# Values of all tokens projected token-major in the first stage, four groups at a time, by way of a scratch in memory; both ends of the last stage reordered

## The reference, cut to what matters

```python
q = (x @ Wq.T).reshape(B, L, H, D)             # x is the normalised input, H = 32, D = 128
k = (x @ Wk.T).reshape(B, L, KVH, D)           # KVH = 8
v = (x @ Wv.T).reshape(B, L, KVH, D)
q, k = _apply_rope(q, cos, sin), _apply_rope(k, cos, sin)
dt = softplus(x @ Win.T + dt_bias); g = dt * -exp(A_log_bias)
G = cumsum(g over a chunk)
scores = q_i . k_j                              # within a chunk of 128 tokens
y_intra = (scores * causal exp(G_i - G_j)) @ (v * dt)
y_inter = (q * exp(G)) @ state before the chunk
state = state * exp(G_last) + (k * exp(G_last - G)).T @ (v * dt)
y = rms_norm(y_intra + y_inter) * gnorm_w * silu(x @ Wg.T)
x1 = x + y @ Wo.T
out = x1 + dense(layer_norm(x1)) + experts(layer_norm(x1))
```

## Time and profile before

| | us |
|---|---|
| median of 3 runs (lowest, highest) | 1906.51 (1904.37, 1909.8) |
| the profiled execution, device time | 1906.53 |
| its span | 1904.7 |
| PE busy | 1824.3 (96%) |
| DVE busy | 1272.7 (67%) |
| ACT busy | 692.1 (36%) |
| POOL busy | 645.5 (34%) |
| mean granted TensorE clock | 0.984 |

### The profile page before, as it was taken

How to read it: one execution, slowest core, us unless ns; L and a number is a source line. 1 busy time by engine, 2 the same in 40 slices (tenths; PEclk the granted TensorE clock), 3 DMA queues, 4 the chain that set the end, 5 groups by cost and what they waited for, 6 DMA issues and landing times. The chain is left out here.

```text
span 1904.7 us, 27787 instructions
## 1 busy us (share of the span) xinstructions
PE 1824.3 (96%) x8856; PEld 1481.1 (78%) x8856; DVE 1272.7 (67%) x2340; ACT 692.1 (36%) x2186; POOL 645.5 (34%) x741
## 2 busy tenths in 40 slices
PE   6799999999999999999999999999887999999997
PEld 4578878877877888787788878888676888888885
DVE  7777877787787778787777868888764333333332
ACT  4534444443344344344444433443442211111111
POOL 3444444444444444444444444444301011010110
PEclk9899999999999999999999999999998999999998
DMA  4132332233233223332322333322364232322321
GB/s 156 46 104 78 99 95 68 71 101 93 82 93 95 70 69 104 96 86 84 95 74 65 106 91 83 87 68 72 129 214 134 82 100 79 98 83 82 100 79 32
DMA packets 111073, 173.54 MB, mean 91 GB/s; under 512 B 8016, under 2 KB 45904, under 8 KB 110928
## 3 DMA queue, kind: packets, MB, share of 16 engines
q1 hardware_dynamic: 110928, 171.80, 30.7%
HBM read 133.50 MB, written 38.27 MB: 90 GB/s over the span
## 5 line engine op out<-in xcount | busy, mean ns | idle before, releaser
L84 PE MATMUL p_proj<-wg_hi,shared 128*128 128x512 f32 x1024 | 360.8, 433 | 0.0
L84 PE MATMUL p_proj<-shared,wq_hi 128*128 128x512 f32 x992 | 335.3, 399 | 0.0
L113 POOL TENSOR_TENSOR q<-rope_a,rope_b 128x512 f32<-128x512 f32 x128 | 166.7, 1302 | 339.7 <-DVE rope_b L105 209.4
L84 PEld LDWEIGHTS p_proj<-wg_hi,shared 128*128 128x128 f32 x1024 | 193.7, 189 | 85.0 <-issue 40.2
L917 ACT ACTIVATE tanh<-p_proj 128x512 f32<-128x512 f32 x128 | 76.5, 598 | 444.8 <-PE p_proj L84 444.8
L84 PEld LDWEIGHTS p_proj<-shared,wq_hi 128*128 128x128 f32 x992 | 186.4, 188 | 44.7 <-issue 1.6
L84 PE MATMUL p_proj<-wg_lo,shared 128*128 128x512 f32 x512 | 203.2, 397 | 0.0
L84 PE MATMUL p_proj<-shared,wq_lo 128*128 128x512 f32 x496 | 196.1, 395 | 0.0
L910 ACT ACTIVATE probs<-g_row,stab 128x128 f32<-128x128 f32 x512 | 164.0, 402 | 54.9 <-POOL g_row L1024 54.8
L694 PE MATMUL p_y<-v_tok,probs 128*128 128x128 f32 x1024 | 182.1, 275 | 0.0
L84 PE MATMUL p_proj<-shared,wkv_hi 128*128 128x512 f32 x496 | 171.4, 407 | 0.0
(11 more groups left out here) (181 smaller groups left out, 3755.5 us busy)
## 6 DMA issues: line engine op xcount, KB each, us to landing
g_row<-g_scratch SPq DMA_DIRECT2D x128, 256.0 KB, 6.0
z_scratch<-z_st SPq DMA_DIRECT2D x256, 128.0 KB
w_raw<-z_scratch SPq DMA_DIRECT2D x63, 512.0 KB, 6.5
e_row<-e_scratch SPq DMA_DIRECT2D x96, 256.0 KB, 4.1
w_raw<-in_wq_t SPq DMA_DIRECT2D x16, 512.0 KB, 8.0
w_raw<-in_wg_t SPq DMA_DIRECT2D x16, 512.0 KB, 5.6
w_raw<-in_wo_t SPq DMA_DIRECT2D x11, 512.0 KB, 5.8
w_raw<-in_wkv_t SPq DMA_DIRECT2D x8, 512.0 KB, 5.1
```

The costliest lines, as they stand in the source:

```text
L84: mm = pe.matmul(out, lhs[a], rhs[e], start=(i == 0 and j == 0), stop=(i == len(pairs) - 1 and j == 2))
L113: pool.tensor_tensor(out, keep["rope_a"][:, s, :], keep["rope_b"][:, s, :], ALU.add).then_inc(keep["roped"], 1)
```

## The change

V is no longer a unit of every attention step. The first stage multiplies each token tile by the V weights of four groups (512 columns) and then by those of the other four, 32 units of 12 matmuls with the tokens on the output's partitions (`values`), saved by ACT (`save_v`) and stored to a scratch in memory (`v_dram`) by SP. The attention stage loads V of a batch and group (256 KB) into one of two buffers, a step ahead (`load_v`); the V unit, `v_turn`, `save_v_rows` and `save_v` of each step are gone. K's weights are loaded and split alone. The first stage's order of loads, splits, table chain and projections is new on all engines, and both tables share one PSUM bank. In the last stage x of tile 0 is loaded first, the last two heads of tile 1 come behind the transposes of tile 0, the splits of W come behind the normalising of tile 0, and `dense` comes behind `turn_hw` and the next tile's heads.

```diff
+        TABLES = 4
+
+        V_LAG, TABLES_AT = 3, 9
+
+        def v_place(v):
+            if v >= 2 * NT - 2:
+                return (keep["k"][:, 1, :], v_tok[:, 1, :, :].rearrange("p c d -> p (c d)"))[v - (2 * NT - 2)]
+            return xin[:, v, :] if v < NT - 2 else v_rows[v % 4]
+
+
+        early_out, place_out = sem("n_early_out"), [sem(f"n_place_out{i}") for i in range(4)]
+
+        def v_count(v):
+            return early_out if v < NT - 2 else place_out[v % 4] if v < 2 * NT - 2 else v_out
...
+            def store_v(v):
+                half, i = v // NT, v % NT
+                sp.wait_ge(v_set, v + 1)
+                sp.dma_start(v_dram[half * HG:(half + 1) * HG, i].rearrange("g s d -> s g d"),
+                             v_place(v).rearrange("p (g d) -> p g d", g=HG)).then_inc(v_count(v), 16)
...
+            for i in (1, 2):
+                sp.dma_start(part(w_raw, i), half_piece(io["wv_t"], 0, i)).then_inc(wv_in[0], 16)
...
             load_x(1)
+            load_x(2)
+            load_x(3)
...
+            sp.dma_start(part(w_raw, 0), k_piece(io, 0)).then_inc(k_in, 16)
+            sp.dma_start(keep["cos"][:, :], io["cos_t"]).then_inc(trig_in, 16)
+            sp.dma_start(keep["sin"][:, :], io["sin_t"]).then_inc(trig_in, 16)
+            sp.wait_ge(wv_lo, 2)
+            for i in (1, 2):
+                sp.dma_start(part(w_raw, i), half_piece(io["wv_t"], 1, i)).then_inc(wv_in[1], 16)
+            for v in range(8):
+                store_v(v)
+            sp.wait_ge(w_lo, 2)
             for i in (1, 2):
                 sp.dma_start(part(w_raw, i), half_piece(io["wq_t"], 0, i)).then_inc(q_in, 16)
-            sp.dma_start(keep["cos"][:, :], io["cos_t"]).then_inc(trig_in, 16)
-            sp.dma_start(keep["sin"][:, :], io["sin_t"]).then_inc(trig_in, 16)
-            sp.wait_ge(w_lo, 3)
+            for v in range(8, NT):
+                store_v(v)
+            sp.wait_ge(w_lo, 5)
             for i in (1, 2):
                 sp.dma_start(part(w_raw, i), half_piece(io["wg_t"], 0, i)).then_inc(g_in, 16)
+            for v in range(NT, NT + TABLES):
+                store_v(v)
             sp.wait_ge(G_set, 1)
             sp.dma_start(g_dram.rearrange("c b g h t -> (b g h) c t"), G[:, :].rearrange("h (c t) -> h c t", t=C)).then_inc(g_out, 16)
             sp.wait_ge(eg_set, 1)
             sp.dma_start(e_dram.rearrange("c b g h t -> (b g h) c t"), eg[:, :].rearrange("h (c t) -> h c t", t=C)).then_inc(g_out, 16)
+            for v in range(NT + TABLES, 2 * NT):
+                store_v(v)
             sp.wait_ge(g_out, 32)
+
+            for i in range(4):
+                sp.wait_ge(place_out[i], 16 * NT // 4)
...
+            w_low(2, wv[1], 1)
+            w_low(3, wv[1], 2)
+            w_low(4, wk, 0)
+            w_low(5, wq, 1)
+            w_low(6, wq, 2)
             add_rope(pool, keep, 0, 0, 0)
-            add_rope(pool, keep, 0, 0, 1)
-            w_low(3, wg, 1)
-            add_rope(pool, keep, 0, 0, 2)
-            w_low(4, wg, 2)
...
                         low_part(i - 2)
-                    if i == 11:
-                        dve.wait_ge(trig_in, 32)
-                        rotate_tile(0)
+                    if i == V_LAG:
+                        for h in (1, 2):
+                            dve.wait_ge(w_hi, h)
+                            dve.tensor_tensor(dst(wv[0][1], h), part(w_raw, h), dst(wv[0][0], h).bitcast(F32),
+                                              ALU.subtract).then_inc(wv_lo, 1)
...
+            def save_v(v):
+                act.wait_ge(v_done, v + 1)
+                if NT + 2 <= v < 2 * NT - 2:
+                    act.wait_ge(place_out[v % 4], 16 * ((v - (NT - 2)) // 4))
+                if v in (NT - 2, NT - 1, NT, NT + 1):
+                    act.wait_ge(xt_done, NT)
+                act.activation(v_place(v), pv[v % 2][:, :], ACT.Copy).then_inc(v_set, 1)
+
             for i in range(NT):
                 halves(i)
-
...
+                if i == 0:
+                    w_high(wv[0], 1, wv_in[0], 32)
+                    w_high(wv[0], 2, wv_in[0], 32)
                 if i == 9:
-                    w_high(wq, 2, q_in, 32)
-                if i == 13:
-                    act.wait_ge(unit_done, 2)
-                    act.activation(keep["v_t"][:, :], p_proj[1][:, :, :].rearrange("p h t -> p (h t)"), ACT.Copy).then_inc(v_set, 1)
+                    w_high(wv[1], 1, wv_in[1], 32)
+                    w_high(wv[1], 2, wv_in[1], 32)
+                if i == 11:
+                    w_high(wk, 0, k_in, 16)
+                    act.wait_ge(small_in, 16 * 2 * B)
+                    act.activation(hcol[:, 2:3], hcol[:, 1:2], ACT.Exp).then_inc(acol_set, 1)
+                if i >= V_LAG:
+                    save_v(i - V_LAG)
+            for v in range(NT - V_LAG, NT):
+                save_v(v)
             act.wait_ge(dt_done, NT)
+            act.wait_ge(early_out, 16 * (NT - 2))
...
-            w_high(wg, 1, g_in, 32)
+            save_v(NT)
             act.wait_ge(u1_set, 1)
...
-            w_high(wg, 2, g_in, 32)
+            save_v(NT + 1)
             act.wait_ge(dt_up_set, 1)
             act.activation(ln_dt[:, :], dt_up[:, :], ACT.Ln).then_inc(ln_dt_set, 1)
+            save_v(NT + 2)
+            w_high(wq, 1, q_in, 32)
+            w_high(wq, 2, q_in, 32)
+            save_v(NT + 3)
             act.wait_ge(G_set, 1)
...
+            for v in range(NT + 4, NT + TABLES_AT):
+                save_v(v)
+            w_high(wg, 1, g_in, 32)
+            w_high(wg, 2, g_in, 32)
             for j, k in enumerate((T_BIAS, T_W)):
                 act.wait_ge(tabs_done, j + 1)
-                act.activation(tab[:, :, k, :], ptab[k][:, :, :], ACT.Copy).then_inc(tabs_saved, 1)
+                act.activation(tab[:, :, k, :], ptab[:, :, :], ACT.Copy).then_inc(tabs_saved, 1)
+            for v in range(NT + TABLES_AT, 2 * NT):
+                save_v(v)
...
+            def values(v):
+                half, i = v // NT, v % NT
+                if i == 0:
+                    if half:
+                        pe.wait_ge(w_lo, 2)
+                    else:
+                        pe.wait_ge(wv_lo, 2)
+                pe.wait_ge(lo_set, i + 1)
+                if v >= 2:
+                    pe.wait_ge(v_set, v - 1)
+                wide(pe, pv[v % 2][:, :], [(x_parts(keep, i // NC, kt, slice(i % NC * P, (i % NC + 1) * P)),
+                                            (wv[half][0][:, kt, :], wv[half][1][:, kt, :])) for kt in range(KT)]).then_inc(v_done, 1)
+
+            def project_tile(r):
+                if r == 0:
+                    pe.wait_ge(w_lo, 3)
+                    pe.wait_ge(lo_set, NC)
+                if r == 1:
+                    pe.wait_ge(w_lo, 5)
+                if r >= 2:
+                    pe.wait_ge(rope_terms, r - 1)
+                project(pe, keep, *((wq, (r - 1) * D) if r else (wk, 0)), 0, p_proj[r % 2]).then_inc(unit_done, 1)
 
             for i in range(NT):
                 turn(i)
                 if i:
                     dt_rows(i - 1)
-                if i == 9:
-                    pe.wait_ge(w_lo, 1)
-                    pe.wait_ge(lo_set, NC)
-                    project(pe, keep, wkv, 0, 0, p_proj[0]).then_inc(unit_done, 1)
-                if i == 12:
-                    project(pe, keep, wkv, D, 0, p_proj[1]).then_inc(unit_done, 1)
+                if i >= V_LAG:
+                    values(i - V_LAG)
             dt_rows(NT - 1)
-            pe.wait_ge(w_lo, 3)
-            for h in range(HG):
-                project_q(h)
+            for v in range(NT - V_LAG, NT + TABLES_AT):
+                values(v)
             for k in (T_BIAS, T_W):
                 turn_table(k)
+            for r in range(ROPED):
+                project_tile(r)
+                values(NT + TABLES_AT + r)
+            for v in range(NT + TABLES_AT + ROPED, 2 * NT):
+                values(v)
...
-        BANKS = (0, 1, 2, 1, 0, 2, 1, 0, 2, 1)
+        BANKS = (0, 1, 2, 0, 1, 2, 0, 1, 2)
...
+            def load_v(g, b):
+                sp.dma_start(v_tok[:, b % 2], v_dram[bass.ds(g, 1), b * NC:(b + 1) * NC].rearrange(
+                    "a c s d -> s (a c) d")).then_inc(v_in[b % 2], 16)
...
+                if ahead(n):
+                    if has_last(n):
+                        sp.wait_ge(y_done, NC * n)
+                    else:
+                        sp.wait_ge(keep["v_out"], 16 * 2)
+                    load_v(g + (b + 1) // B, (b + 1) % B)
...
                     k_turn(n + 1, b + 1)
-                next_unit(g, b, n, V_UNIT)
-                mix(n, 3)
-                if ahead(n):
-                    v_turn(n + 1)
+                mix(g, b, n, 3)
                 first_heads(n, range(4, HP))
...
                 if c == 0:
-                    pool.wait_ge(tok_saved, 2 * n + 2)
+                    pool.wait_ge(v_in[b % 2], v_loads(g, b))
...
```

(70 more changed lines are left out.)

178 lines of the change are left out of this document (79 added, 99 removed).

## The result

The changed kernel takes 2016.20 us, the median of 4 runs (2009.75 to 2023.16), where the kernel before takes 1905.44 beside it: 1.058 times as long (interval 1.056 to 1.060). The prediction said slower, 1976 us and at most 2000; the direction was right, the size too small by 40 us. The profiled execution of the changed kernel took 2009.75 us, its span is 2007.9 and its granted clock 0.962 (before: 0.984).

What follows compares the result with a forecast made beforehand. With less PE work, VectorE's chain at each attention step's end was taken to bound the attention stage. Span 1904.7 + 93 (first stage) - 15 (attention) - 9 (last stage) = 1973.7, plus 1.8: 1976 us, range 1940 to 2000.

Steps and rivals of the forecast that it cites:

- The tail on DVE: End of each attention step: DVE's unedited chain of 10.2 us ends last, making the step 39.4 us.
- the collision: In DVE's chain: k_lo takes 1.27 us beside GpSimd's sum and stays so; otherwise the step would be 38.8 us.
- the forecast of this stage (-15): Attention steps 0 to 30, now 1280.3 us: a gain of 15 us with 12 clock falls in 24 steps.
- ScalarE loses two copies: Attention step: two copies of 0.6 us go from ScalarE, which ends nothing there since its q_high waits for GpSimd.
- The clock: Attention steps: a pause of about 2.15 us lowers PE's clock in half of 24 steps, 1.6 us a fall.
- Rival (2): Attention stage: every pause lowers PE's clock, giving 1995 us in all; chance 0.27.
- Steps with b = 0: Seven attention steps that load q weights, where GpSimd waits for the row of G: 41.3 us, bounds 39.4 and 42.8.
- PE's work: Each attention step: PE loses 3.2 us and its own work becomes 37.1 us, but the step gains only 0.95 us.
- First stage: Added value units and waits: attention starts at 167 us instead of 73.90, +93 us, bounds +60 and +100.
- Rival (4): First stage: SyncE's order of stores and loads doesn't hold PE up, 13 us less; no separate chance given.
- Last stage: New order after attention: 7 us of PE pauses and 2 of low clock go, 9 us, bounds 4 and 11.
- the rival on the other side: Attention stage stays bounded by PE, DVE's tail under 7.9 us, steps 37.1 us: 1887 us in all; chance 0.06.

Runs made afterwards that it cites:

- xw later: Changed kernel, with GpSimd's first weighted V of a step (xw for chunk 0) made to wait for DVE's q_lo: 1988.07 us, ratio 1.0436.
- the stores first: Changed kernel, with SyncE issuing the stores of value units 16 to 19 ahead of its wait for q-weight splits and the gate weights: 2004.86 us.

## Why the prediction was wrong in size

**The tail on DVE.** The step that failed is the last sentence on the collision: "The two keep their distance after the change, so it stays". That was said of k_lo, and there it held (1.27 us before, 1.23 after). I had looked only at GpSimd's instruction inside the tail. The next one in its order, xw, waited for ScalarE's copy of V, and the change removes that copy; its start jumps to the end of the last mask, right onto q_lo. So the tail is 11.0 us and not 10.2: 0.8 us in each of 31 steps, 25 us of the 35 between the forecast of this stage (-15) and the trace (+19.8). The run with xw later shows it by undoing it. The edit was in my own list of what goes ("ScalarE loses two copies"), costed at nothing because it ends nothing on ScalarE; I did not ask who waited for them. The page SBUF — State Buffer of the Trainium skill ("Who interferes with whom") has the exclusive lock on the ports that VectorE and GpSimd share; q_lo at 1.53 us beside xw and 0.68 without agrees with it.

**The clock.** This term of the sum was mis-sized: I took 19 falls of 1.6 us, 30 us. In the changed kernel there were 24 steps with the low clock, and together they lost 44 us to it: sixteen of them 1.3 to 1.6 us each, eight between 2.3 and 2.8. That is 14 of the 35 us. Rival (2), every pause lowers the clock, is what the run with xw later shows for the very pause that I forecast, about 2.1 us: 30 of 31. It had 0.27 of my chances, and its 1995 us is the changed kernel without the collision (1988). More rows of the kernel before would not have warned me: of its pauses ahead of V's transposes those of 2.13 to 2.30 us (behind steps 8, 12, 20 and 24) all have a low-clock step behind them, those of 1.66 and 1.90 none. It is the later runs in which the length of the pause doesn't decide. That a pause of 4 us always lowers the clock, which the sum used without a row, came true in all seven of 3.8 to 4.4 us.

**Steps with b = 0.** Without the low clock's share the seven take 42.7 us (step 0) and 41.1 to 41.7, 41.6 in the mean, where I had 41.3 with the shorter tail. They gave back some 3 us against the sum, which closes it: 24.8 + 13.6 - 3.4 = 35.0 us. Nothing was run for this term alone.

**PE's work, and the two ways the stage can be bounded.** Right: 37.1 us of PE's own work (37.11 measured), 29.1 us to the start of the tail, and that the tail takes over, so that 3.2 us of work removed from PE bring nothing.

**First stage.** Right to 4 us of 93. The values start at 21.96 us (forecast 23.4), a tile takes 33.71 - 29.29 = 4.42, PE stands still for 7.8 us at unit 20 for the reason given, and the run with the stores first puts the whole of this at 10.4 us with the cold start, where the sum had 10 and 1.5. Rival (4), that SyncE's order doesn't bite, is refuted. DMA: Bandwidth & Descriptors of the Trainium skill ("Queues, rings and completion order") has each DMA engine take a queue's descriptors in ring order; the store of unit 16, issued 0.9 us behind 1 MB and waited for till 111.7, agrees.

**Last stage.** -5.6 us from S31 on, where I took -9 within -4 to -11. The last stage alone is 6.7 us shorter (507.10 to 500.40), and in the run with only the new last stage everything from S31 on is 7.0 shorter; the other 1.1 us is step 31, at the low clock in the changed kernel. The two pauses of the earlier trace rows did nearly go. In the run with only the new last stage 0.57 us are left ahead of the transposes, and 1.04 us of a wait have come ahead of the transpose of hwn (p_hwt), which in the kernel before waited 0.3 us in all. What else keeps this from 9 us was not followed.

The range, 1940 to 2000, had the rivals one by one. It needed one more that made the tail longer: the rival on the other side asked what happens if the tail is under 7.9 us, none what happens if it grows.

## What to carry to other kernels

When a change removes a wait, follow the waiting engine's next instruction to its new place and ask what runs there: a step that costs nothing where it is removed can start another on top of the critical chain. When two engines' chains are nearly as long, taking work from one is worth only the slack between them (here 1.1 us of 3.2), until work that waits for nothing is put into the pause; here the order of two lines was worth 104 us to the changed kernel and nothing to the kernel before, whose pause stood elsewhere. And before a costly move of work is judged, both sides should have the cheap re-orderings: with them the two places of V came out at 1879 us each.

## What the runs showed of the hardware

- TensorE's lower clock came in 22 of the 23 steps behind a pause of 2.0 us (xw later), and in 23 of the 30 behind pauses of 2.8 us and more (changed kernel); seven of the longer ones left it up, and so did one of 2.26 us behind step 8 of the kernel before with the new last stage. The length of the pause alone does not decide it, and what does is open. The slow matmuls can begin up to 1.5 us after work has begun again (xw later, 0.3 to 1.5 us in 26 of its steps), at matmuls that nothing else disturbs.
- The usual fall costs 1.5 us of a step (40.90 against 39.4, xw later), with a granted clock of 0.75 and 0.80 in the 7.75 us behind S of its step 7; in eight steps of the changed kernel the low clock took 2.3 to 2.8 us.
- Ten matmuls that compute nothing of use, in each pause, made a kernel 2% faster (1973.12 against 2016.20 us) and brought the granted clock from 0.962 to 0.986.
- A DVE instruction of 128x512 took 0.68 us alone and 1.53 beside one GpSimd instruction of 1.03 us: it lost 0.85 of the 0.97 us in which they overlapped.
